# Cross-attention and a mixture of gated units on one core: first stacks by TensorE, first weights through ScalarE's queue, own slot offsets for the first half, value products by twos

## The chip, the cores and the metric

The kernel runs on one core of one Trainium2 chip. TensorE (PE) multiplies and transposes, VectorE (DVE), ScalarE (ACT) and GpSimd (POOL) do the element-wise work, and DMAs are issued here from SyncE's queue (SP), after the change from ScalarE's as well. Each engine runs its own list of instructions in order and waits on semaphores. The metric is the device time of one execution in microseconds (us), lower is better.

## The reference

One layer on x (4 batches of 512 tokens, 512 features), in float32. First attention: 16 query heads of 32 features in 4 groups, each group with one key and value head read from a 128-wide context; the queries come from the normalised x, both sides go through an RMS norm and a rotary embedding, the mask is causal, and the result is projected and added to x. Then a mixture: a router picks 4 of 128 experts per token, eight gated units are mixed with the experts' weights, two shared units are added, all goes through a down projection and is added again.

```python
q, k = _rms_norm(q, q_norm_w), _rms_norm(k, k_norm_w)      # then split into heads
q = q * cos + _rotate_half(q) * sin                        # k likewise
scores = einsum('bgnqd,bgkd->bgnqk', qg, k) * scale        # causal, then softmax
x = x + (attn @ v) @ w_out.T
gate, up = xt @ w_gate, xt @ w_up                          # 8 units of 256 columns, 2 shared
basis = silu(gate) * up                                    # mixed over the 4 chosen experts
x = x + mixed @ w_down + shared
```

## The kernel before

The program is written by hand on a grid of **slots**, from FIRST = -32 to LAST = 236. Each engine's function loops over the slots and issues, in a fixed order within a slot, the steps that tables of numbers assign to it. Nothing is scheduled at run time: the order of an engine is this list, and a late semaphore holds up all that stands behind it.

**Attention** is cut into spans `u`: a batch, a half of 256 queries (h = 0 or 1) and one of the 4 key heads, 32 spans in all. A span of half 0 takes 4 slots and has 2 steps over keys, one of half 1 takes 6 to 8 slots and has 4 steps. The constants `CORE` give each step of a span its slot, counted from the span's first.

- *Preparation.* A tile n is one 128-wide block of 256 tokens, keys first and then four query tiles for each half (n = 0 keys, n = 1 to 4 the queries of spans u = 0 to 3, n = 5 the keys of half 1, and so on). POOL (for the first two tiles partly DVE, `rope_start`) weighs it and makes the rotary parts r1_b and r2_b; POOL adds them (`rope_last`, L669); PE turns the tile by two transposes (`turn_in`, L1177); ACT rounds the turned tile to its high part (`turned_high`, L752); DVE takes the low part, the rest (`turned_low`, L933).
- *Stacking.* The scores are computed with three products in one, so each head needs its high, high and low rows (keys: high, low, high) one above the other in 96 rows of q_st or k_st. `stack_keys` (L490) and `stack_queries` (L500) do this with 12 DMAs a tile on SP's queue.
- *First pass* (`pass_a`, L1205): 8 score tiles, whose row minimum (scores are negated) DVE takes (L945) and whose exponentials ACT sums (L766). The maxima are split, turned and moved by 2 DMAs into rows 96 and 97 of q_st (`rows`, L508); rows 96 and 97 of k_st are ones (`memset`, L877).
- *Second pass* (`pass_b`, L1217 and L1220), transposed scores with the maxima subtracted, ACT's exponential (L781) into one of 3 buffers, then `value_product` (L1232): four heads at a time, 32 columns of the array each.
- `q_st` has 3 buffers, so `stack_queries(u)` waits for the second pass of u-3.

**The fillers** are the large products of projection, units and down projection (L1299, L1314, L1334), one per slot from slot 20 on. Their weights come in chunks of 1 MB into 3 buffers by DMAs on SP's queue, and are split into high and low parts by ACT (L738), DVE (L1000) and, for one block in four, POOL (L699).

**SP's queue** also carries all loads and stores. The first three chunks, the router's weights and two small tables are issued behind the query stack of u = 0; the second batch's context and x and the resident weights behind that of u = 2.

Of the kernel before, what the change touches and what calls it, by code (L numbers as in the profile page):

```python
# [13 lines left out]
CORE = dict(split=-1, inverse=2, maxima=0, spread=4, second_pass=3, inverse_turn=5,  # L14
            values=5, high=1)
# [3 lines left out]
PREP = dict(key_squares=(-31, -8), key_scale=(-24, -2), query_scale=(-24, 2), key_rope=(-21, 2),  # L19
            key_turn=(-18, 5), key_stack=(-16, 8))  # L20
SPLIT = dict(high=(3, 2), low=(2, 1))
MOMENTS = (-30, -29, -4, -4)
CONTEXT = -46
# [4 lines left out]
TILE_AT = dict(scales=(1, 3), normalize=(2, 4), turn_x=(4, 5), route=(6, 7))  # L28
PAIR_AT = dict(choose=8, keep=9, coefficients=9, turn_choice=10, mix=12)
# [20 lines left out]
def attention_and_mixture_kernel(nc, x, ctx_in, q_norm_w, k_norm_w, w_out, w_router, w_units, w_down,  # L50
# [31 lines left out]
    H = 2  # L82
# [5 lines left out]
    W8, W9 = NK, NK + 1  # L88
    POOL_LOW = (3,)
# [8 lines left out]
    with common:  # L98
# [29 lines left out]
        th, gb = sb("th", [P, 2, I]), sb("gb", [P, 2, I])  # L128
        d_h, d_l = sb("d_h", [P, 2, ND * P], F32R), sb("d_l", [P, 2, ND * P], F32R)
# [35 lines left out]
        s_tab = sem("tables_landed")  # L165
# [83 lines left out]

        def of_span(s, name):  # L250
            return spans.get(s - CORE[name])

        def second_pass_step(s):
            for u in range(NU):
                k = s - span_slot(u) - CORE["second_pass"]
                if 0 <= k < steps(u):
                    return u, k
            return None

        def value_step(s):  # L260
            for u in range(NU):
                k = s - span_slot(u) - CORE["values"]
                if 0 <= k < steps(u):
                    return u, k
            return None

        def attended_in(s):
            step = value_step(s)
            return step[0] if step and step[1] == steps(step[0]) - 1 else None
# [9 lines left out]
        def of_query(s, name):  # L279
            for u in range(NU):  # L280
                if s == span_slot(u - 2) + QUERY[name]:
                    return u
            return None
# [10 lines left out]

        spans = {span_slot(u): u for u in range(NU)}
# [49 lines left out]
        def keys_in(u):  # L345

            b, h, kv = span(u)
            c = b * KV + kv
            return [(s_k[c % KR][i], 48 * (c // KR + 1)) for i in range(h + 1)]

        def queries_in(u, j):
            return s_q[u % QR][j], 48 * (u // QR + 1)
# [7 lines left out]
        def stacked(n):  # L360

            hb, i = n // NB, n % NB
            if i == 0:
                c = hb // H * KV
                return [(s_k[(c + j) % KR][hb % H], 48 * ((c + j) // KR + 1)) for j in range(KV)]
# [48 lines left out]

        def short_products(s):

            found = []
            if (u := of_query(s, "turn")) is not None:
                found.append(("turn", query_tile(u)))
            if (hb := of_half(s, "key_turn")) is not None:  # L420
                found.append(("turn", hb * NB))
# [5 lines left out]
            if (u := of_span(s, "inverse_turn")) is not None:  # L427
                found.append(("inverse", u))
            if (g := mixture(s, "turn_x")) is not None:
                found.append(("x", g))  # L430
            if (g := turned_down(s)) is not None:
                found += [("down", 2 * g), ("down", 2 * g + 1)]
            found += [("scores", u * G * TH + m) for u, m in first_pass_tiles(s)[1:]]
            if (p := routing(s, "turn_choice")) is not None:
                found.append(("choice", p))
            if (p := routing(s, "mix")) is not None:
                found.append(("mix", p))
# [12 lines left out]
        def short_free(kind, i):  # L450
# [4 lines left out]
            return short_read[shorts[n][0]], shorts[n][1] + 1  # L455
# [3 lines left out]
        def sync_engine(e):  # L459
# [11 lines left out]

            def load_chunk(i):
                p, w = chunks[i]
                if i >= WR:
                    e.wait_ge(*chunk_read(i - WR))
                src = w_out if w == "wo" else shared_w_down if w == "ws" else w_units[w]
                for h in range(2):
                    e.dma_start(w_raw[:, i % WR, 2 * h:2 * h + 2, :], src[:, 2 * h:2 * h + 2, :]
                                ).then_inc(s_chunk[i % WR][h], 16)
# [37 lines left out]
            for t in range(TT):  # L517
                e.dma_start(x1[:, t, :], x[0, t * P:(t + 1) * P, :]).then_inc(s_x0[t], 16)
                if t == 1:
                    e.dma_start(cos_t[:], rope_cos.rearrange("(t p) d -> p t d", p=P)).then_inc(s_tab, 16)  # L520
                    e.dma_start(sin_t[:], rope_sin.rearrange("(t p) d -> p t d", p=P)).then_inc(s_tab, 16)
                    e.dma_start(wk_b[:], k_norm_w.partition_broadcast(P)).then_inc(s_tab, 16)
                    e.dma_start(wq_b[:], q_norm_w.partition_broadcast(P)).then_inc(s_tab, 16)
            for s in slots:
                if (hb := of_half(s, "key_stack")) is not None:
                    stack_keys(hb)
                for i in range(WR, len(chunks)):
                    if s == chunk_slot[i - WR] + 2:
                        load_chunk(i)
# [7 lines left out]
                for b in range(2, B):  # L537
                    if s == batch_slot(b) + CONTEXT:
                        load_ctx(b)
                if (u := of_query(s, "stack")) is not None:  # L540
                    stack_queries(u)
                    if u == 0:
                        load_chunk(0)
# [901 lines left out]
```

## Time and profile before

| | us |
|---|---|
| median of 3 runs | 898.04 (895.24 to 898.12) |
| the profiled execution | 898.34 |
| its span, first to last instruction | 896.3 |
| PE busy | 812.5 (91%) |
| DVE busy | 647.9 (72%) |
| ACT busy | 576.3 (64%) |
| POOL busy | 503.3 (56%) |

The span is what the trace covers; 2.0 us of the profiled execution lie around it. Busy is the time in which an engine has an instruction under way. Instructions on SP are issues of DMAs: the time of one is that of issuing, not of the transfer.

### The profile page before, as it was taken

To read this page: it belongs to the slowest core of one execution; us is meant where nothing else is said; L and a number is where in the kernel's file an instruction comes from. 1 tells how busy PE (TensorE), PEld (TensorE's weight loads), DVE (VectorE), ACT (ScalarE), POOL (GpSimd) and SP (SyncE) were. 2 spreads that over 40 slices of the span, in tenths; PEclk is the share of its full clock that TensorE was granted. 3 is DMA by queue.
4 is the path that set the end of the run, shared out by engine and by line. 5 is a ranking of instruction groups with operands and counts; after the bars stand their busy time and mean duration, and the time that the engine had idled before them with its cause. 6 is when DMAs were issued, how large, how long until landed. Compare 5 with 4: busy or idle time off the path is not lost. (4 is left out here: it accounts for less than half of the span.)

```text
span 896.3 us, 15336 instructions
## 1 busy us (share of the span) xinstructions
PE 812.5 (91%) x4224; PEld 602.1 (67%) x4224; DVE 647.9 (72%) x1627; ACT 576.3 (64%) x1412; POOL 503.3 (56%) x686
## 2 busy tenths in 40 slices
PE   0276978999999999999999999999999999999997
PEld 0143556767777687666777677767777777778885
DVE  3234676778887886688877786777878776678674
ACT  0265687767777676567687675667687775555452
POOL 6634551896348851797338952797345532662471
PEclk9975788999999999999999999999999999999999
DMA  3543113444453454554544453454444444454551
GB/s 95 191 128 92 58 48 112 156 140 140 153 170 123 163 159 150 174 182 136 162 145 143 163 162 128 150 171 137 160 147 144 146 141 149 158 188 141 191 192 41
DMA packets 60163, 128.37 MB, mean 143 GB/s; under 512 B 12848, under 2 KB 31152, under 8 KB 60080
## 3 DMA queue, kind: packets, MB, share of 16 engines
q1 hardware_dynamic: 60080, 127.39, 43.6%
q8 instruction: 36, 0.59, 0.3%
q14 instruction: 47, 0.39, 0.1%
HBM read 107.16 MB, written 4.19 MB: 124 GB/s over the span
## 5 line engine op out<-in xcount | busy, mean ns | idle before, releaser
L1314 PE MATMUL u<-w_h,t_h 128*128 128x512 f32 x640 | 260.7, 407 | 6.4 <-POOL w_l L699 5.6
L1314 PE MATMUL u<-w_h,t_l 128*128 128x512 f32 x640 | 251.5, 393 | 0.0
L1314 PE MATMUL u<-w_l,t_h 128*128 128x512 f32 x640 | 251.2, 393 | 0.0
L1000 DVE TENSOR_TENSOR w_l<-w_raw,w_h 128x512 fp32r<-128x512 f32 x288 | 246.0, 881 | 0.0
L738 ACT ACTIVATE w_h<-w_raw 128x512 fp32r<-128x512 f32 x384 | 219.1, 621 | 20.8 <-DMA w_raw<-in_w_units 20.2
L699 POOL TENSOR_TENSOR w_l<-w_raw,w_h 128x512 fp32r<-128x512 f32 x96 | 140.7, 1465 | 132.3 <-ACT w_h L738 131.9
L945 DVE CUSTOM_DVE_ANT_0 scores<-s,mask_qk 128x128 f32<-128x128 f32 (+3 forms) x256 | 123.5, 487 | 105.0 <-PE s L1205 102.9
L766 ACT ACTIVATE scores<-scores,mx 128x128 f32<-128x128 f32 (+3 forms) x256 | 142.4, 558 | 74.9 <-DVE mx L945 73.5
L707 POOL TENSOR_TENSOR macc<-macc,gb 128x256 f32<-128x256 f32 x112 | 103.7, 926 | 72.1 <-DVE gb L1101 71.2
L1314 PEld LDWEIGHTS u<-w_h,t_h 128*128 128x128 f32 x640 | 121.6, 190 | 32.5 <-POOL w_l L699 8.6
L1314 PEld LDWEIGHTS u<-w_h,t_l 128*128 128x128 f32 x640 | 120.7, 189 | 26.7
L1314 PEld LDWEIGHTS u<-w_l,t_h 128*128 128x128 f32 x640 | 121.3, 189 | 21.3
L1205 PE MATMUL s<-k_st,q_st 96*128 96x256 f32 (+2 forms) x256 | 102.9, 415 | 17.5 <-issue 16.6
L781 ACT ACTIVATE pr<-pair 128x1024 f32<-128x1024 f32 x96 | 84.3, 878 | 31.1 <-PE pair L1220 26.0
L828 ACT ACTIVATE th<-u 128x256 f32<-128x256 f32 x160 | 59.7, 373 | 55.0 <-PE u L1314 54.2
L1082 DVE SCALAR_TENSOR_TENSOR th<-th,u 128x256 f32<-128x256 f32 x160 | 66.7, 417 | 38.3 <-ACT th L828 37.8
L675 POOL TENSOR_TENSOR o_l<-att,o_h 128x256 fp32r<-128x256 f32 x32 | 25.8, 807 | 121.2 <-ACT o_h L786 121.2
L1205 PEld LDWEIGHTS s<-k_st,q_st 96*128 96x128 f32 x256 | 52.8, 211 | 54.8 <-issue 49.9
L1217 PE MATMUL pair<-q_st,k_st 98*128 98x512 f32 x160 | 64.3, 458 | 18.3 <-DMA q_st<-m_t 11.8
L1101 DVE SCALAR_TENSOR_TENSOR gb<-th,wt,u 128x256 f32<-128x256 f32 x112 | 53.9, 481 | 16.3 <-DVE th L1082 0.5
L1232 PE MATMUL o_bank<-pr,ct 128*32 128x256 f32 (+1 forms) x768 | 57.5, 373 | 0.0
L766 ACT ACTIVATION_READ_ACCUMULATOR scores<-scores,mx 128x1 f32 x256 | 48.7, 190 | 0.0
(139 smaller groups left out, 1148.6 us busy)
## 6 DMA issues: line engine op xcount, KB each, us to landing
w_raw<-in_w_units SPq DMA_DIRECT2D x160, 512.0 KB, 4.2
q_st<-turned_h SPq DMA_DIRECT2D x256, 32.0 KB, 1.9
w_raw<-in_w_out_t SPq DMA_DIRECT2D x16, 512.0 KB, 4.0
w_raw<-in_shared_w_down SPq DMA_DIRECT2D x16, 512.0 KB, 4.6
q_st<-turned_l SPq DMA_DIRECT2D x128, 32.0 KB, 1.9
out<-x SPq DMA_DIRECT2D x16, 256.0 KB, 2.0
x<-in_x SPq DMA_DIRECT2D x3, 1024.0 KB, 5.9
k_st<-turned_h SPq DMA_DIRECT2D x64, 32.0 KB, 1.9
```

The costliest lines, as they stand in the source:

```text
L699: e.tensor_tensor(w_l[:, i % WR, k, :], w_raw[:, i % WR, k, :], f32(w_h[:, i % WR, k, :]), ALU.subtract).then_inc(s_wlp, 1)
L707: e.tensor_tensor(total, total, gb[:, adds_before(w, g) % 2, :], ALU.add).then_inc(s_acc, 1)
L738: e.activation(w_h[:, i % WR, k, :], w_raw[:, i % WR, k, :], ACT.Copy).then_inc(s_wh, 1)
L766: e.activation(s, s, ACT.Exp, bias=mx[:, u % 2, t, j:j + 1], scale=-1.0, accum_out=sums[:, u % 2, t, j:j + 1]).then_inc(s_sum, 1)
L781: e.activation(pr[:, n % PR, 0:width], pair[:, 0:width], ACT.Exp, scale=-1.0).then_inc(s_ex, 1)
L828: e.activation(th[:, n % 2, :], u_bank[filler_no[f] % 2][:, 0:I], ACT.Tanh, scale=0.5).then_inc(s_tanh, 1)
L945: e.tensor_tensor_reduce(scores[:, i % AR, 0:width], short("scores", i)[:, 0:width], mask_qk[:, T - width:T], 1.0, 3e38, ALU.add, ALU.min, ...
L1000: e.tensor_tensor(w_l[:, i % WR, k, :], w_raw[:, i % WR, k, :], f32(w_h[:, i % WR, k, :]), ALU.subtract).then_inc(s_wl, 1)
L1082: e.scalar_tensor_tensor(th[:, n % 2, :], th[:, n % 2, :], 1.0, up, ALU.add, ALU.mult).then_inc(s_ga, 1)
L1205: e.matmul(short("scores", i)[:, 0:w], q_st[0:MAXROW, u % QR, j, t * P:(t + 1) * P], k_st[0:MAXROW, (b * KV + kv) % KR, 0:w], start=True, ...
L1217: last = e.matmul(dst, k_st[:, (b * KV + kv) % KR, k * P:(k + 1) * P], q_st[:, u % QR, i * n:(i + 1) * n, Q - w:Q], start=True, stop=True)
L1314: last = e.matmul(u_bank[n % 2][:], t[:, k, cols], ww[:, i % WR, k, :], start=(k == 0 and m == 0), stop=(k == KC - 1 and m == 2))
```

## The change

- **First stacks by TensorE.** For tiles n = 0 to 3 (`U0 = 3`: keys of half 0 and the queries of u = 0, 1, 2) POOL's last addition goes; DVE adds r1_b and r2_b and writes the sum three times side by side (`rope_stacked`, 768 elements a partition). PE makes 8 transposes of 96 columns (`turn_stacked`), which come out stacked in two banks. ACT copies each bank into q_st or k_st (`stacked_high`), DVE overwrites the low rows (`stacked_low`, two subtractions). The 12 DMAs of each of these tiles are gone, and readers wait for `s_tl` instead.
- **Queues.** The first three chunks, router, resident weights and the small tables are issued by ACT, after x's second tile has landed. SP issues k_norm_w before the tables, has own semaphores for it and q_norm_w, and issues the second batch's context and x at once, the third's x at slot 15.
- **Offsets.** Spans of the first half (u < 4) take their slots from `LEAD`, others from `CORE`, of which `inverse`, `spread` and `values` change. Some numbers of `PREP`, `MOMENTS`, `TILE_AT` and `PAIR_AT` move by a few slots. The ones of k_st are set at slot -9 and not first.
- **Value products by twos** (`value_products`): two steps over keys follow each other directly, in the slot in which the second of them stood before (in the first half of batch 0, in the slot of the first). Their semaphore rises by 2 at the end of the pair.
- Within a slot the steps stand in another order on PE, ACT, DVE and POOL, and the second of two tiles that read the same chunk no longer waits for the chunk's splitting.

```diff
-CORE = dict(split=-1, inverse=2, maxima=0, spread=4, second_pass=3, inverse_turn=5,
-            values=5, high=1)
+CORE = dict(split=-1, inverse=1, maxima=0, spread=2, second_pass=3, inverse_turn=5,
+            values=6, high=1)
+
+LEAD = dict(split=-1, inverse=0, maxima=1, spread=0, second_pass=3, inverse_turn=3, values=5, high=0, rope=-11, turn=0, stack=-3)
...
+CONTEXT, ONES = -44, -9
+ROPE3 = (-20, -11, -6, -4)
+LOADS = (-1, 15)
...
+        def queries_in(u, j):
+            if u < U0:
+                return s_tl, u + 2
+            return s_q[u % QR][j], 48 * sum(i % QR == u % QR for i in range(U0, u + 1))
...
+            def stacked_high(n):
+                e.wait_ge(s_turn, n + 1)
+                for i in range(2):
+                    last = e.activation(stack_of(n, i), short("stack", 2 * n + i)[0:MAXROW, :].rearrange(
+                        "p (j q) -> p j q", j=2), ACT.Copy)
+                last.then_inc(s_th, 1)
...
+            def rope_stacked(n):
+                e.wait_ge(*cosined(n))
+                e.wait_ge(s_rs, n + 1)
+                if n >= 2:
+                    e.wait_ge(s_turn, n - 1)
+                parts = (part.rearrange("p t (h d) -> p (t h) d", d=D).unsqueeze(2).broadcast_to([P, TH * G, 3, D])
+                         for part in (r1_b[:, n % 2], r2_b[:]))
+                e.tensor_tensor(r3[:, n % 2], *parts, ALU.add).then_inc(s_rope, 1)
...
+            def stacked_low(n):
+                rows = slice(D, 2 * D) if n == 0 else slice(2 * D, 3 * D)
+                e.wait_ge(s_th, n + 1)
+                for i in range(2):
+                    low = stack_of(n, i)[rows]
+                    last = e.tensor_tensor(low, short("stack", 2 * n + i)[rows, :].rearrange("p (j q) -> p j q", j=2),
+                                           f32(low), ALU.subtract)
+                last.then_inc(s_tl, 1)
...
+            def turn_stacked(n):
+                e.wait_ge(s_rope, n + 1)
+                e.wait_ge(s_mask, 1)
+                for i in range(2):
+                    e.wait_ge(*short_free("stack", 2 * n + i))
+                    bank = short("stack", 2 * n + i)
+                    for j in range(2):
+                        for t in range(TH):
+                            copies = r3[:, n % 2, t * G + 2 * i + j].rearrange("p c d -> p (c d)")
+                            last = e.transpose(bank[0:MAXROW, j * Q + t * P:j * Q + (t + 1) * P], copies, ident[:])
...
-            def value_product(u, k):
+            def value_products(u, first):
                 b, h, kv = span(u)
-                n, w = step_no(u, k), Q - seen(u, k)
-                e.wait_ge(s_ex, n + 1)
-                if k == 0:
+                if first == 0:
                     e.wait_ge(s_att, u)
...
+                for k in (first, first + 1):
+                    n, w = step_no(u, k), Q - seen(u, k)
+                    e.wait_ge(s_ex, n + 1)
...
+                last.then_inc(s_pv, 2)
```

On SP's queue, the stretch from the query stack of u = 2 to that of u = 3, before. `q_st<-m_t` are the rows of maxima.

```order
L500 DMA q_st<-turned_l 32x256
L508 DMA q_st<-m_t 1x4x256 [waits max_out]
L508 DMA q_st<-m_t 1x4x256
L500 DMA q_st<-turned_h 32x256 [waits turned_low]
L500 DMA q_st<-turned_h 32x256
L500 DMA q_st<-turned_l 32x256
```

The same queue after, from the last loads at the start to the first keys that still go by DMA (those of half 1).

```order
L512 DMA ct<-in_ctx 128x4x128
L518 DMA x<-in_x 128x4x512
L548 DMA q_st<-m_t 1x4x256 [waits max_out]
L548 DMA q_st<-m_t 1x4x256
L540 DMA q_st<-turned_h 32x256 [waits pass_b,turned_low]
L540 DMA q_st<-turned_h 32x256
L540 DMA q_st<-turned_l 32x256
```

The first stacks by DMA are now those of u = 3, behind the first rows of maxima and behind a wait for the second pass of u = 0; before, four tiles and all loads stood ahead of them.

On DVE, from the second tile's cosine part to the first row minimum, before (`ISA` of L888 is a sum of squares, that of L945 the row minimum).

```order
L927 TENSOR_TENSOR r_b<-rw_b,csq 128x256 [waits q_tables_dve,weighed_dve]
L933 TENSOR_TENSOR turned_l<-s,turned_h 128x256 [waits turned_high]
L888 ISA junk,ssk<-ct 128x128 [waits key_squares,ctx0_landed]
L888 ISA ssk 128x1
L888 ISA junk,ssk<-ct 128x128 [waits key_squares,ctx0_landed]
L888 ISA ssk 128x1
L933 TENSOR_TENSOR turned_l<-s,turned_h 128x256 [waits turned_high]
L945 ISA scores,mx<-s,mask_qk 128x128 [waits masks_set,pass_a]
```

The same place and what follows it, after (L987 is the cosine part, L999 the threefold addition, L1011 the low rows, L1024 the row minimum).

```order
L987 TENSOR_TENSOR r_b<-rw_b,csq 128x256 [waits q_tables_dve,weighed_dve]
L1011 TENSOR_TENSOR k_st<-s,k_st 32x2x256 [waits turned_high]
L1011 TENSOR_TENSOR k_st<-s,k_st 32x2x256
L999 TENSOR_TENSOR r<-r_b 128x768 [waits sine,cosine_dve]
L936 MEMSET k_st 2x3072
L1011 TENSOR_TENSOR q_st<-s,q_st 32x512 [waits turned_high]
L1011 TENSOR_TENSOR q_st<-s,q_st 32x512
```

```order
L1024 ISA scores,mx<-s,mask_qk 128x128 [waits masks_set,pass_a]
L1024 ISA mx 128x1
L1011 TENSOR_TENSOR q_st<-s,q_st 32x512 [waits turned_high]
L1011 TENSOR_TENSOR q_st<-s,q_st 32x512
L1024 ISA scores,mx<-s,mask_qk 128x256 [waits masks_set,pass_a]
L1024 ISA mx 128x1
L999 TENSOR_TENSOR r<-r_b 128x768 [waits turned,sine,cosine_pool]
```

The low rows and the additions of the next query tiles now stand between the row minima of u = 0, each behind a wait for PE and ACT.

On PE, in the last two slots of a span of half 1, before: two steps of value products with a score tile between them.

```order
L1232 MATMUL o_bank<-pr,ct 32x256 x4
L1205 MATMUL s<-k_st,q_st 128x384
L1232 MATMUL o_bank<-pr,ct 32x128 x4
L1205 MATMUL s<-k_st,q_st 128x512
```

After, the same two steps.

```order
L1308 MATMUL s<-k_st,q_st 128x512
L1336 MATMUL o_bank<-pr,ct 32x256 x4
L1336 MATMUL o_bank<-pr,ct 32x128 x4
L1308 MATMUL s<-k_st,q_st 128x384
```

They now stand next to each other.

## Rows read from the trace of the kernel before

**Rows 1.** The page: PE's busy share, in tenths, in 40 slices of the span.

```profile
PE   0276978999999999999999999999999999999997
```

**Rows 2.** Busy time by stretch: us, PE, PEld, DVE, ACT, POOL, PEclk, DMA, GB/s.

```profile
60.00:70.00 10.00, 8.24 (x36) 4.45 (x36) 4.45 (x23) 6.33 (x22) 1.56 (x4) 0.50 0.20 52
...
200.00:300.00 100.00, 98.18 (x532) 73.52 (x530) 81.94 (x207) 74.14 (x184) 61.16 (x84) 1.00 0.47 154
```

**Rows 3.** The timeline of SP, 42 to 91 us: start, us, line, tiles.

```profile
42.39 1.36 SPq L508 DMA_DIRECT2D q_st<-m_t  x2
...
54.49 1.20 SPq L500 DMA_DIRECT2D q_st<-turned_h  x2
...
70.18 1.29 SPq L508 DMA_DIRECT2D q_st<-m_t  x2
...
79.17 0.58 SPq L469 DMA_DIRECT2D x<-in_x  x1
79.85 1.28 SPq L508 DMA_DIRECT2D q_st<-m_t  x2
...
90.17 1.28 SPq L508 DMA_DIRECT2D q_st<-m_t  x2
```

**Rows 4.** The timeline of PE where the second passes start, 60 to 100 us.

```profile
72.65 0.79 PE L1217 MATMUL pair<-q_st,k_st 98*128 98x512 f32 x1 [3.65 <-DMA q_st<-m_t]
...
98.61 1.19 PE L1217 MATMUL pair<-q_st,k_st 98*128 98x512 f32 x2 [2.06 <-ACT pr L781]
```

**Rows 5.** The timeline of all engines, 3 to 35 us.

```profile
10.24 0.23 DVE L907 TENSOR_TENSOR csq<-cos_t,sc 128x64 f32<-128x64 f32 x1 [3.64 <-DMA wq_b<-in_q_norm_w]
...
13.05 0.69 PE L1177 MATMUL s<-ident,r_b 128*128 128x128 f32 x2 [13.05 <-POOL r_b L669]
...
25.48 0.77 PE L1205 MATMUL s<-k_st,q_st 96*128 96x256 f32 x2 [3.14 <-issue]
...
34.12 0.37 ACT L758 ACTIVATE m_t<-s 8x256 fp32r<-8x256 f32 x1 [0.62 <-PE s L1185]
```

**Rows 6.** The same view, 75 to 115 us: second pass, splitting of weights, low parts.

```profile
85.56 0.80 PE L1217 MATMUL pair<-q_st,k_st 98*128 98x512 f32 x1 [3.21 <-DMA q_st<-m_t]
...
94.23 1.14 ACT L738 ACTIVATE w_h<-w_raw 128x512 fp32r<-128x512 f32 x2
...
94.74 1.05 PE L1217 MATMUL pair<-q_st,k_st 98*128 98x512 f32 x2
...
95.72 1.66 DVE L1000 TENSOR_TENSOR w_l<-w_raw,w_h 128x512 fp32r<-128x512 f32 x2
...
114.90 0.69 DVE L1014 TENSOR_TENSOR t_l<-s,t_h 128x512 fp32r<-128x512 f32 x1 [0.54 <-ACT t_h L799]
```

**Rows 7.** The timeline of PE around value products and without them, 606 to 621 us.

```profile
606.98 0.39 PE L1299 MATMUL u<-w_h,o_l 128*128 128x512 f32 x1
607.29 0.43 PE L1232 MATMUL o_bank<-pr,ct 128*32 128x128 f32 x8
607.65 0.38 PE L1205 MATMUL s<-k_st,q_st 96*128 96x256 f32 x1
607.87 0.40 PE L1314 MATMUL u<-w_h,t_h 128*128 128x512 f32 x1
...
609.02 0.39 PE L1314 MATMUL u<-w_h,t_l 128*128 128x512 f32 x1
...
609.37 0.40 PE L1314 MATMUL u<-w_h,t_h 128*128 128x512 f32 x1
...
619.58 0.39 PE L1314 MATMUL u<-w_h,t_l 128*128 128x512 f32 x1
...
620.69 0.38 PE L1194 MATMUL s<-ident,rrep 128*128 128x128 f32 x2
```

**Rows 8.** One line's instructions over 95 to 896 us: the value products.

```profile
L1232 PE MATMUL o_bank<-pr,ct x704: 272/379/636, 103.7 to 770.8; 128*32 128x256 f32 x120, 128*32 128x128 f32 x56
```

**Rows 9.** Waits of PE over the span: us in total, times, longest.

```profile
PE u L1314 <- POOL w_l L699: 5.6, 7, 1.7
```

More of the change, by code:

```diff
@@ L258, in second_pass_step, with value_steps, attended_before @@
             return None
-        def value_step(s):
+        def value_steps(s):
             for u in range(NU):
-                k = s - span_slot(u) - CORE["values"]
-                if 0 <= k < steps(u):
-                    return u, k
+                for k in range(0, steps(u), 2):
+                    if s == span_slot(u) + core(u, "values") + k:
+                        return u, k
             return None
         def attended_in(s):
-            step = value_step(s)
-            return step[0] if step and step[1] == steps(step[0]) - 1 else None
+            found = value_steps(s)
+            return found[0] if found and found[1] == steps(found[0]) - 2 else None
+        def attended_before(s):
+            for u in range(NU):
+                if s == span_slot(u) + core(u, "values") + steps(u) - 2 + core(u, "high"):
+                    return u
+            return None
         def first_pass_tiles(s):
@@ L348, in keys_in, with keys_half_in @@
             c = b * KV + kv
-            return [(s_k[c % KR][i], 48 * (c // KR + 1)) for i in range(h + 1)]
+            return [keys_half_in(c, i) for i in range(h + 1)]
+        def keys_half_in(c, h):
+            if c < KV and h == 0:
+                return s_tl, 1
+            earlier = range(KV if h == 0 else 0, c + 1)
+            return s_k[c % KR][h], 48 * sum(i % KR == c % KR for i in earlier)
         def queries_in(u, j):
-            return s_q[u % QR][j], 48 * (u // QR + 1)
+            if u < U0:
+                return s_tl, u + 2
+            return s_q[u % QR][j], 48 * sum(i % QR == u % QR for i in range(U0, u + 1))
         def max_rows(u):
@@ L411, in evicted, with stacks @@
             return gated(w, g)
+        def stacks(n):
+            return [("stack", 2 * n), ("stack", 2 * n + 1)] if n <= U0 else [("turn", n)]
         def short_products(s):
             found = []
[L418 to L421, printed above, removed]
             if (u := of_span(s, "maxima")) is not None:
@@ L454, in short_free, with stack_of, load_chunk @@
                 return s_mask, 1
-            return short_read[shorts[n][0]], shorts[n][1] + 1
+            kind, i = shorts[n]
+            return (s_tl, i // 2 + 1) if kind == "stack" else (short_read[kind], i + 1)
+        def stack_of(n, i):
+            if n == 0:
+                return k_st[0:MAXROW, 2 * i:2 * i + 2, 0:Q]
+            return q_st[0:MAXROW, n - 1, 2 * i:2 * i + 2, :]
+        def load_chunk(e, i):
+            p, w = chunks[i]
+            if i >= WR:
+                e.wait_ge(*chunk_read(i - WR))
+            src = w_out if w == "wo" else shared_w_down if w == "ws" else w_units[w]
+            for h in range(2):
+                e.dma_start(w_raw[:, i % WR, 2 * h:2 * h + 2, :], src[:, 2 * h:2 * h + 2, :]
+                            ).then_inc(s_chunk[i % WR][h], 16)
         def sync_engine(e):
@@ L876, in vector_engine, with ones @@
         def vector_engine(e):
-            e.memset(f32(k_st[MAXROW:ROWS, :, :]), 1.0).then_inc(s_ones, 1)
+            def ones():
+                e.memset(f32(k_st[MAXROW:ROWS, :, :]), 1.0).then_inc(s_ones, 1)
             def key_squares(hb):
```

276 lines of the change are left out of this document (154 added, 122 removed).

## The prediction

> **What bounds the kernel now.** I read four views. The 40 slices of the span first: PE is nearly idle at the start, half busy in slices 3 to 5 and at 9 tenths from slice 6 on [rows 1]. Each slice is 22.4 us, so there are two regimes. Then the busy times by stretch: from 200 to 300 us PE has 98.18 of 100 us at clock 1.00, the others 61 to 82; from 60 to 70 us it has 8.24 of 10 at clock 0.50, the lower of its two levels, 1.2 GHz [rows 2]. From about 100 us on PE's own stream is the bound. Before that something else is.
>
> What, is in SP's timeline. From the first key stack to the rows of span 4 SP issues one DMA after another, about 0.6 us each (two in 1.20 to 1.36), back to back but for the last microsecond. The rows of maxima of spans 0, 2, 3 and 4 are issued at 42.39, 70.18, 79.85 and 90.17 [rows 3]. Those of span 0 had been ready in m_t since 34.12 + 0.37 = 34.5 [rows 5]: they stood 8 us behind weights and stacks. PE in turn waits for exactly these rows in its second passes, 3.65 us at 72.65 and 3.21 at 85.56 [rows 4, 6]. The head is bound by SP's issuing. How long rows take to arrive depends on what was queued: 2.5 us from 70.18 to 72.65, 5.7 us from 79.85 to 85.56 with a load of x issued just before, at 79.17 [rows 3, 4, 6].
>
> **The head.** The change takes 48 stacking DMAs (4 tiles of 12) and the first weights off SP. It doesn't follow that their 30 us go, since in their place comes a chain through four engines, and I follow it.
>
> Keys. PE began to turn them at 13.05 [rows 5]. DVE now adds 768 elements where POOL added 256. No row shows that. Two additions of 512 elements took 1.66 us [rows 6], 0.83 each; 768 cost between that and 1.5 times it, and I take 1.2. PE starts at about 13.4. Eight transposes for two: two took 0.69 [rows 5]; four times that is 2.8, but they overlap, so I take 2.0. ACT's two copies of 512 columns take 1.14 as the two of the weights [rows 6], DVE's two low parts read a bank as the row of 0.69 does [rows 6], 1.3. With gaps the keys are complete at 18.2. Before, twelve issues of 0.6 us, 7.6 us, followed the turn.
>
> Queries of span 0. Their addition stands on DVE behind the keys' low rows: 18.2 + 1.2 + 2.0 + 1.2 + 1.3 and gaps gives 24.3. The first score tile came at 25.48 [rows 5] and now comes at about 24.5. The chain thus gives back nearly all that the DMAs cost. The ones of k_st (2.6 us of DVE) are now set while PE and ACT turn this tile, so they cost nothing as long as that takes 3.2 us; uncovered they would cost 2.6. The loads that moved: x, context and weights are some 5 MB that now start in the first 12 us. In the profile DVE waited 3.64 us for q_norm_w, to 10.24 [rows 5]. It is now needed at about 13.8, so contention has 3 us to use up before it costs. ACT's ten issues, at 0.6 each and behind x's second tile, end by 13, before its first copy at 15.5.
>
> First pass of span 0. On DVE the order now puts span 1's low rows behind the first row minimum, span 2's addition behind the second and span 2's low rows into span 1's first pass. Each waits for addition, PE, ACT in turn, 4.5 us and gaps. From 24.5: sums of squares and addition to 27, low rows of span 1 done at 31.6, addition to 33, six row minima and a moment to 37, the turn of span 2 (its bank must be free) 38, low rows 40.7, and only then the maxima's transposes, which need that bank: m_t at 42. Before it was 34.5. **The rows of span 0 leave at 42.3 where they left at 42.39.** Bounds: if none of this lies between, the maxima follow the first tile by 34.5 - 25.5 = 9.0 us as before, 33.5; if nothing overlaps, 46.
>
> From there the gain begins. No load is under way, so these rows arrive in 2.5 us (bound 5.7). The second pass of span 0 takes some 4 us with one exponential in between, and releases the stacks of span 3, which wait for it: at 48.8, where they began at 54.49 [rows 3]. From here to the rows of span 4 SP has the same 36 us in both: 48 stacks at 0.635, three pairs of rows at 1.4, one load; before, 90.17 - 54.49 = 35.7. So they leave at 84.5, not 90.17. The load of x now stands right before them, so I give them the slow 5.3 to 5.7 us, and the second pass of span 4 begins at about 90, not 94.74 [rows 6]. **Term: -5 us**; from -14 (33.5 for 42.3) to 0 (46, or a slow landing).
>
> The Trainium skill, page "DMA: Bandwidth & Descriptors", section "Issuing engines are not separate DMA queues", says that issuing from another engine saves only the time to initiate a DMA, usually small against the transfer. Here rows 3 show that time, 0.6 us a piece without a gap, as the bound of the head. By the page the head would give nothing.
>
> **Value products by twos.** Between a product's last matmul at 606.98 and the next unit's at 607.87 lie 0.89 us with a value step and one score tile; with the score tile alone, 609.02 to 609.37, it is 0.35 [rows 7]. So a step of 128 columns costs 0.54. One of 256 costs 620.69 - 619.58 - 0.35 = 0.76 [rows 7]. Twice the columns cost 0.22 more, so some 0.3 us of every step are not columns: entering and leaving the narrow tiles. From 95 us on there are 704 / 8 = 88 steps [rows 8], afterwards 44 pairs, and each pair enters and leaves once: 44 x 0.3 = 13 us. The eight steps before 95 us lie beside SP and give nothing. No row shows two steps side by side, so the bounds are 0 (each step still pays) and 14.
>
> The page "TensorEngine Tiling (Array Packing)", section "Key Properties", of the Trainium skill says that changing the tiling mode, not just the tile, drains TensorE. That would make the cost one of the pair. By it the sum is the 13 us; if every new tile paid, it would be 0.
>
> Not all of it arrives. PE also waits after 100 us, mostly short and for others: 5.6 us in 7 waits for POOL's w_l in the units [rows 9]. What PE wins just ahead of such a wait, the wait takes back. **Term: -11 us.**
>
> **The rest.** The orders within a slot, the slots of choose, turn_x, inverse and spread, and the dropped waits move work on engines that are 61 to 82% busy beside PE at 98% [rows 2]. I set them at 0. The slack of a slot (3.6 us) covers each; uncovered, one such place costs what POOL's longest wait does, 1.7 us [rows 9]. PE idles 1.8 us in 100 there [rows 2], so some 14 us in 800 are to be had, or to be added to: -6 to +6.
>
> **Sum.** 898.3 of the profiled execution - 5 - 11 = 882.3; it stands 0.3 above the median, so 882.
>
> **Rivals.**
> *The chain hides* (0.20). PE may have turned to its upper clock level by the first stacks, which shortens eight transposes to about 1 us each time, and DVE may overlap more. Then the rows of span 0 leave at 33.5 to 38 and the head gives 10 to 14: 898.3 - 14 - 11 = 873. Against it: at 60 to 70 us PE, much busier, still had 0.50 [rows 2].
> *The head gives nothing* (0.15), which is what the page on DMA would say: the chain ends at 46 or the loads delay a norm weight: 887.
> *Pairs don't pay* (0.13): the drain belongs to each step, or waits take the gain: 893 with the head's 5.
> *Slower* (0.06). The exponential of a span's fourth step writes the buffer of its first, which is released only with the pair, one slot later than before; the next second pass waits for that exponential. PE lost 2.06 us in such a wait at 98.61 [rows 4]. The 16 us of gain are gone from the eighth such stall; one in each of the 16 spans of half 1 costs 33: 898.3 - 16 + 33 = 915. Against it: the pair stands early in the slot, the exponential late.
>
> **Numbers.** The forecast, 877 to 888, has 0.42. 868 to 893 leaves out the far end of the first rival (0.06) and what is above (0.12), and takes in the bounds of head and pairs one at a time. 0.3% is what a measurement can tell from no change, 2.7 us: faster by more 0.90 (the forecast and three rivals), within it 0.04 (pairs and head both without effect), slower 0.06.
>
> **What would show it.** Rows of span 0 leaving SP near 42 us, stacks of span 3 near 49, the rows of span 4 near 84 and PE dense from 95 instead of 100. In value products, sixteen matmuls together and 0.3 us less in each pair. Wrong would be: rows of span 0 before 38 (head too small), a gap between the two steps of a pair, or new PE waits for `pr` or w_l of more than 2 us that recur with the batch.

## The result and the profile after

The change makes the kernel faster: 876.39 us (median of 4 runs, 875.83 to 878.02) against 898.08 us; the ratio is 0.9768, with a 95% interval of 0.9744 to 0.9792. That is 20.8 us less by the ratio, where 16 were forecast; 876.4 lies inside the range of 868 to 893 and below the forecast's own 877. The profiled execution took 878.02 us, with a span of 876.2.

The page of the kernel after answers to [rows 1]: PE's busy share in 40 slices of 21.9 us.

```profile
span 876.2 us, 15366 instructions
...
PE   1566789989999998989999999998999999999997
```

PE now works in the first slice and is at 9 from the seventh on, with a few 8s among them, where before the steady 9 began with the eighth. The first projection (88.59, below) still comes only at the end of the fourth slice. The prediction reads slices 3 to 5 of [rows 1] as half busy and a 9 from the sixth on; they show 7, 6 and 9. No term of its sum rests on that.

SP's timeline after, 39 to 83 us, answers to [rows 3] (L548: rows of maxima, L540: query stacks, L518: load of x).

```profile
39.41 1.36 SPq L548 DMA_DIRECT2D q_st<-m_t  x2
46.17 1.22 SPq L540 DMA_DIRECT2D q_st<-turned_h  x2
...
54.64 1.28 SPq L548 DMA_DIRECT2D q_st<-m_t  x2
...
81.47 0.58 SPq L518 DMA_DIRECT2D x<-in_x  x1
82.18 1.27 SPq L548 DMA_DIRECT2D q_st<-m_t  x2
```

The rows of span 0 leave at 39.41 (before 42.39), the stacks of span 3 at 46.17 (before 54.49), the rows of span 4 at 82.18 (before 90.17). Between the last two it took 36.0 us, before 35.7, but the two are not made of the same. Before there were two pairs of rows between and SP stood idle for 1.4 us ahead of the rows of span 4, whose maxima ACT finished only at 90.15. After there are three pairs and next to no gap, and these maxima had been ready since 80.44, 1.7 us before their turn. The lines are SP's last stack and ACT's copy of the maxima before, then ACT's copy after.

```profile
88.16 0.59 SPq L500 DMA_DIRECT2D q_st<-turned_l  x1
89.79 0.36 ACT L758 ACTIVATE m_t<-s 8x256 fp32r<-8x256 f32 x1
```

```profile
80.08 0.36 ACT L801 ACTIVATE m_t<-s 8x256 fp32r<-8x256 f32 x1
```

The timeline of DVE after, 11 to 37 us, shows the chain that took the DMAs' place (L999: threefold addition, L936: the ones, L1011: low rows).

```profile
11.48 0.96 DVE L999 TENSOR_TENSOR r<-r_b 128x768 f32<-128x768 f32 x1 [1.62 <-POOL r_b L697]
...
16.86 1.28 DVE L1011 TENSOR_TENSOR k_st<-s,k_st 32x512 fp32r<-32x512 f32 x2 [3.17 <-ACT k_st L793]
18.17 0.96 DVE L999 TENSOR_TENSOR r<-r_b 128x768 f32<-128x768 f32 x1
19.83 2.62 DVE L936 MEMSET k_st<- 2x3072 f32 x1 [0.70 <-issue]
22.48 1.29 DVE L1011 TENSOR_TENSOR q_st<-s,q_st 32x512 fp32r<-32x512 f32 x2
...
28.56 1.29 DVE L1011 TENSOR_TENSOR q_st<-s,q_st 32x512 fp32r<-32x512 f32 x2 [2.00 <-ACT q_st L793]
...
36.73 1.29 DVE L1011 TENSOR_TENSOR q_st<-s,q_st 32x512 fp32r<-32x512 f32 x2 [1.84 <-ACT q_st L793]
```

And PE's timeline of the same stretch and up to the first filler, with the stack of transposes (L1280), score tiles (L1308), second passes (L1320) and the projection (L1404).

```profile
12.49 1.95 PE L1280 MATMUL s<-ident,r 128*96 128x128 f32 x8 [12.49 <-DVE r L999]
...
23.87 0.55 PE L1308 MATMUL s<-k_st,q_st 96*128 96x256 f32 x1 [2.74 <-DVE q_st L1011]
...
41.96 0.79 PE L1320 MATMUL pair<-q_st,k_st 98*128 98x512 f32 x1 [0.49 <-DMA q_st<-m_t]
...
57.09 0.80 PE L1320 MATMUL pair<-q_st,k_st 98*128 98x512 f32 x1 [5.94 <-DMA q_st<-m_t]
...
87.30 1.17 PE L1320 MATMUL pair<-q_st,k_st 98*128 98x512 f32 x2 [2.47 <-DMA q_st<-m_t]
88.27 0.52 PE L1308 MATMUL s<-k_st,q_st 96*128 96x384 f32 x1
88.59 0.63 PE L1404 MATMUL u<-w_h,o_h 128*128 128x512 f32 x1
...
91.00 0.63 PE L1320 MATMUL pair<-q_st,k_st 98*128 98x512 f32 x2
```

The first score tile comes at 23.87 (before 25.48), the second pass of span 4 at 87.30 (before 94.74).

For the kernel before, the same view shows the first projection at 99.60, behind a second pass that had waited for the exponential:

```profile
99.60 0.63 PE L1299 MATMUL u<-w_h,o_h 128*128 128x512 f32 x1
```

So of the 20.1 us between the two spans, 7.4 are won up to the second pass of span 4, 3.6 between that and the first projection (4.9 us before, 1.3 after), and 9.1 from there to the end. The 3.6 are not all gain. The wait for the exponential that is gone took 2.06 of them; the other 1.5 are work that now stands behind the first projections and no longer ahead of them, above all the two matmuls of the second step, at 98.61 before [rows 4] and at 91.00 after. So some 2 us were won there and 10.6 behind it.

A pair of value products after, between a score tile and a unit, answers to [rows 7]:

```profile
587.77 0.28 PE L1308 MATMUL s<-k_st,q_st 96*128 96x256 f32 x1
587.98 0.86 PE L1336 MATMUL o_bank<-pr,ct 128*32 128x256 f32 x16
588.77 0.50 PE L1420 MATMUL u<-w_h,t_h 128*128 128x512 f32 x1
589.11 0.39 PE L1420 MATMUL u<-w_l,t_h 128*128 128x512 f32 x1
```

Sixteen matmuls stand in one group. From 587.77 to 589.11 it is 1.34 us; a score tile and a unit's matmul alone take 0.35 ([rows 7]), so both steps cost 0.99, where a step of each size on its own cost 0.54 + 0.76 = 1.30. A pair is 0.31 us cheaper, as computed from one place of each kernel. The waits in the units, answering to [rows 9], from 100 to 870 us:

```profile
PE u L1420 <- POOL w_l L735: 7.6, 5, 2.7
PE u L1420 <- DVE gb L1180: 3.3, 1, 3.3
...
PE u L1404 <- POOL w_l L735: 2.2, 2, 1.5
```

PE waits longer for POOL than before: 7.6 for 5.6 us in the units. The longest two of these waits are

```profile
394.80 0.80 PE L1420 MATMUL u<-w_h,t_h 128*128 128x512 f32 x1 [2.67 <-POOL w_l L735]
...
593.93 0.50 PE L1420 MATMUL u<-w_h,t_h 128*128 128x512 f32 x1 [2.68 <-POOL w_l L735]
```

They stand 199 us apart, and the longest in the units before was 1.7 us [rows 9].

### The profile page after: what moved, and what is told of

Its sections match the earlier page's. It is cut to its first block, busy times and chain, and to the rows that moved or that the text cites. A ratio compares the mean times of both kernels' runs of the same rounds, so it can differ in the third digit from the quotient of the medians.

```text
span 876.2 us, 15366 instructions
## 1 busy us (share of the span) xinstructions
PE 803.1 (92%) x4248; PEld 614.5 (70%) x4248; DVE 655.1 (75%) x1635; ACT 576.3 (66%) x1416; POOL 502.6 (57%) x682
## 4 chain that ended last, share of the span: by engine, by line
PE 60%; POOL 14%; SPq 6%; issue 6%; DVE 6%; ACT 3%; DMA 3%; ACTq 1%; POOLq 0%; DVEq 0%
PE u L1420 36%; PE u L1441 7%; SPq L540 4%; PE pair L1320 3%; PE o_bank L1336 3%; PE s L1308 3%; POOL macc L743 3%; POOL w_l L735 2%; PE u L1404 2%; POOL r_b L697 2%; PE pair L1323 1%; PE s L1356 1%; PE s L1388 1%; DVE w_l L1079 1%; DMA w_raw<-in_w_units 1%
## 5 line engine op out<-in xcount | busy, mean ns | idle before, releaser
L1420 PE MATMUL u<-w_h,t_h 128*128 128x512 f32 x640 | 267.1, 417 | 11.5 <-POOL w_l L735 7.6
L1079 DVE TENSOR_TENSOR w_l<-w_raw,w_h 128x512 fp32r<-128x512 f32 x288 | 248.7, 890 | 0.9 <-ACT w_h L774 0.9
L735 POOL TENSOR_TENSOR w_l<-w_raw,w_h 128x512 fp32r<-128x512 f32 x96 | 134.8, 1404 | 130.4 <-ACT w_h L774 130.2
L1024 DVE CUSTOM_DVE_ANT_0 scores<-s,mask_qk 128x128 f32<-128x128 f32 (+3 forms) x256 | 123.4, 486 | 87.9 <-PE s L1308 85.6
L743 POOL TENSOR_TENSOR macc<-macc,gb 128x256 f32<-128x256 f32 x112 | 112.6, 1007 | 56.6 <-DVE gb L1180 55.9
L1308 PE MATMUL s<-k_st,q_st 96*128 96x256 f32 (+2 forms) x256 | 94.5, 380 | 12.3 <-DVE q_st L1011 5.1
L1320 PE MATMUL pair<-q_st,k_st 98*128 98x512 f32 x160 | 62.7, 448 | 11.0 <-DMA q_st<-m_t 9.3
L1308 PEld LDWEIGHTS s<-k_st,q_st 96*128 96x128 f32 x256 | 52.5, 209 | 28.2 <-issue 13.1
L711 POOL TENSOR_TENSOR o_l<-att,o_h 128x256 fp32r<-128x256 f32 x32 | 23.8, 743 | 83.2 <-ACT o_h L829 83.2
L809 ACT ACTIVATION_READ_ACCUMULATOR scores<-scores,mx 128x1 f32 x256 | 48.8, 190 | 0.0
L1336 PE MATMUL o_bank<-pr,ct 128*32 128x256 f32 (+1 forms) x768 | 47.2, 366 | 0.0
```

What stands on the lines that cost most here:

```text
L735: e.tensor_tensor(w_l[:, i % WR, k, :], w_raw[:, i % WR, k, :], f32(w_h[:, i % WR, k, :]), ALU.subtract).then_inc(s_wlp, 1)
L743: e.tensor_tensor(total, total, gb[:, adds_before(w, g) % 2, :], ALU.add).then_inc(s_acc, 1)
L809: e.activation(s, s, ACT.Exp, bias=mx[:, u % 2, t, j:j + 1], scale=-1.0, accum_out=sums[:, u % 2, t, j:j + 1]).then_inc(s_sum, 1)
L1024: e.tensor_tensor_reduce(scores[:, i % AR, 0:width], short("scores", i)[:, 0:width], mask_qk[:, T - width:T], 1.0, 3e38, ALU.add, ALU.min, ...
L1079: e.tensor_tensor(w_l[:, i % WR, k, :], w_raw[:, i % WR, k, :], f32(w_h[:, i % WR, k, :]), ALU.subtract).then_inc(s_wl, 1)
L1308: e.matmul(short("scores", i)[:, 0:w], q_st[0:MAXROW, u % QR, j, t * P:(t + 1) * P], k_st[0:MAXROW, (b * KV + kv) % KR, 0:w], start=True, ...
```

## The experiments

Each kernel was timed in turn with the kernel before on the same chip; ratios are to that. Repeated executions of one kernel differ by 0.2 to 1% here, so a milestone of a single profile is read beside the median, not for it. The kernels ran on more than one chip, where the kernel before took 897.9 to 899.2 us; differences of medians below can therefore be off by about 1 us, and where one matters the difference by the ratios stands beside it, with its 95% interval (an estimate from the two intervals).

**Value products: undone, alone, and with POOL out of the way.** The kernel `single` is that of after with single steps, the second in its place:

```diff
-            values=6, high=1)
+            values=5, high=1)
...
-                for k in range(0, steps(u), 2):
+                for k in range(steps(u)):
...
-                for k in (first, first + 1):
+                for k in (first,):
```

> The kernel after, with each value step on its own again (the first of a pair one slot earlier, the second where the pair stands). If entering and leaving the narrow tiles costs 0.3 us a step, 44 more of these after 88 us cost up to 13 us: 889. The kernel after spends 8.7 us less from the first projection on than before, so if waits swallow part, 885. If the pairs are worth nothing and the other order did it all: 876.

Measured: 882.86 us (ratio 0.9828, 0.9805 to 0.9852), 6.5 us more than after, or 5.4 by the ratios (2 to 8). It is nearer to the 885 of partly swallowed pairs than to 889. The expectation's 8.7 us from the first projection on should read 9.1. `before_pairs` is the kernel before with the two steps written together in `value_product`, at the second's slot:

```diff
+                if second % 2 == 0:
+                    return
...
+                for k in (second - 1, second):
+                    n, w = step_no(u, k), Q - seen(u, k)
+                    e.wait_ge(s_ex, n + 1)
...
-                last.then_inc(s_pv, 1)
+                last.then_inc(s_pv, 2)
```

> The kernel before, with pairs of value steps and nothing else. Pairs worth 11 us on their own: 887. If they need the other orders to be of use: within 2 us of 898. The start up to the second pass of span 4 stays at 94.7 us.

Measured: 893.81 us (ratio 0.9961, 0.9935 to 0.9987): 4 us less than before, and neither 887 nor nothing. The ten executions fall into seven from 891.7 to 894.8 and three from 898.2 to 900.5, and the profile is of one of the three; in it the second pass of span 4 begins at 94.53, as before. Both kernels say that half or less of the 13 us arrives. The waits of PE from 100 to 870 us in the profile of `single` say where the rest may be:

```profile
PE u L1420 <- POOL w_l L735: 4.5, 4, 1.9
PE u L1420 <- DVE gb L1180: 2.9, 1, 2.9
...
PE u L1404 <- POOL w_l L735: 1.4, 2, 0.7
```

With single steps PE waits 5.9 us for POOL's w_l, with pairs 9.8, and all its waits of this stretch together grow from some 21 to 26 us. To test that, the next two kernels leave POOL's low part of each chunk's fourth block out, and PE multiplies by the high part in its place; one has pairs, one single steps.

```diff
             if k in POOL_LOW:
-                return s_wlp, i * len(POOL_LOW) + sum(j in POOL_LOW for j in range(k + 1))
+                return s_wh, i * KC + k + 1
...
-                    for m, (t, ww) in enumerate(((t_h, w_h), (t_h, w_l), (t_l, w_h))):
+                    for m, (t, ww) in enumerate(((t_h, w_h), (t_h, w_h if k in POOL_LOW else w_l), (t_l, w_h))):
```

> Leaves work out: POOL no longer makes the low part of a chunk's fourth block, and TensorE multiplies by the high part in its place (same number of matmuls, another result). With pairs. PE's 9.8 us of waits for POOL's w_l go, and POOL is freer: 862 to 868. To be read against the next kernel.

> The same with single value steps. If the pairs' 13 us are partly swallowed by waits for POOL's w_l, the difference to the kernel with pairs, 6.5 us with POOL's work in place, grows to 10 to 13 here. If a pair itself is worth only half of what I computed, it stays at 6.5.

Measured: 857.99 us with pairs, 870.41 with single steps. The first is below the 862 to 868 expected. The difference is 12.4 us (10 to 15 by the ratios), where it was 6.5 with POOL's work in place. So pairs are worth nearly the 13 us computed, and POOL's low parts took about half of that back. The profiles agree in direction, with smaller numbers: from the first projection to the end pairs give 9.5 us without POOL's low parts (89.70 to 857.9 for 91.35 to 869.0) and 3.6 with them (88.59 to 876.2 for 89.65 to 880.9). Taking POOL's low parts away gave 18.4 with pairs and 12.4 with single steps, more than the waits for w_l, 9.8 and 5.9. POOL has some 135 us less to do, and behind a wait PE's matmuls run slower for a while (a filler's matmul every 0.42 us behind the wait at 394.80, every 0.23 ahead of 587.77); how the 18.4 divide between these was not tested.

**Stacks by TensorE, undone.**

```diff
-    U0 = 3
+    U0 = -1
...
-            if c < KV and h == 0:
-                return s_tl, 1
-            earlier = range(KV if h == 0 else 0, c + 1)
+            earlier = range(c + 1)
```

> The kernel after, but all stacks by DMA again (48 issues more on SP, no transposes of 96 columns). My theory: the chain through DVE, PE and ACT costs nearly what the DMAs did; rows of span 0 leave SP near 45 us for 39.4, stacks of span 3 near 51 for 46.2, the time rises by 5 us to 881. Rival: the 30 us of issuing were on the path, 900 or more.

Measured: 883.72 us (ratio 0.9831, 0.9796 to 0.9865), 7.3 more than after, or 5.7 by the ratios (2 to 10). SP's timeline of this kernel:

```profile
45.40 1.35 SPq L546 DMA_DIRECT2D q_st<-m_t  x2
...
62.35 1.28 SPq L546 DMA_DIRECT2D q_st<-m_t  x2
...
91.11 1.28 SPq L546 DMA_DIRECT2D q_st<-m_t  x2
```

The rows of span 0 leave at 45.4, as expected, 6 us later than after and not 30. The stacks of span 3 begin at 54.77, where 51 was expected, and the rows of span 4 leave 8.9 us later than after. The chain costs nearly what the DMAs did, and the theory of the head stands; its size in the total stays rough, since the profiled execution (879.53) is the fastest of four that reach 885.48, and made up most of the 9 us behind the first projection.

**Queues.** `loads_on_sp` issues the first weights and small tables from SP at the start:

```diff
-            e.wait_ge(s_x0[1], 16)
-            load_chunk(e, 0)
...
+            load_chunk(e, 0)
+            e.dma_start(rt_raw[:, :, NE:2 * NE], w_router).then_inc(s_rt, 16)
```

> The kernel after, but the first weights, router and small tables issued by SP at the start. SP is idle from about 7 to 39 us in the kernel after, so ten more issues cost nothing: 876 within 1.5. If issuing by ACT or its own queue is what helps, 880 or more.

Measured: 874.81 us (ratio 0.9738, 0.9711 to 0.9766): no loss, at most a small gain; the intervals of the two overlap. It is not ScalarE's queue that helps. Its profile shows what the issues on ACT cost in the kernel after. With the loads on SP, ACT loads its table at 0.72 and copies the keys as soon as PE has turned them:

```profile
0.72 1.28 ACT L800 ACT_TABLE_LOAD   x1 [0.72 <-PEq L1546]
15.31 1.08 ACT L800 ACTIVATE k_st<-s 96x512 fp32r<-96x512 f32 x2 [13.31 <-PE s L1279]
```

In the kernel after, the table load of 1.28 us stands behind the ten issues and begins at 14.45, just when the eight transposes end (12.49 + 1.95). The copy has to wait for it until 15.74:

```profile
14.45 1.28 ACT L793 ACT_TABLE_LOAD   x1 [14.45 <-issue]
15.74 1.08 ACT L793 ACTIVATE k_st<-s 96x512 fp32r<-96x512 f32 x2
```

So the issues on ACT put 1.3 us into the chain of the keys. With the loads on SP the first turn begins 0.84 us later (13.33), and still the first score tile comes 0.44 earlier (23.43). In `before_act_loads` the kernel before gets the change's move of the loads alone, ten issues from SP to ACT:

```diff
                     stack_queries(u)
-                    if u == 0:
-                        load_chunk(0)
-                        e.dma_start(rt_raw[:, :, NE:2 * NE], w_router).then_inc(s_rt, 16)
...
-                        load_chunk(1)
-                        load_chunk(2)
...
         def scalar_engine(e):
...
+            e.wait_ge(s_x0[1], 16)
+            load_chunk(0)
+            e.dma_start(rt_raw[:, :, NE:2 * NE], w_router).then_inc(s_rt, 16)
+            load_chunk(1)
+            e.dma_start(wd_raw[:], w_down).then_inc(s_wd, 16)
```

> The kernel before, with only the first weights, router and small tables issued by ACT at the start. SP loses ten issues, 6.5 us, ahead of the stacks of span 3. If SP's issuing is the bound of the head, these leave it near 48 instead of 54.5 and the time falls by 6 us, to 892. If the head is bound by something else, or these loads now slow the stacks, 898.

Measured: 893.40 us (ratio 0.9953, 0.9931 to 0.9974), 4 to 5 us less. The stacks of span 3 begin at 50.48, not 48. The first rows of maxima leave SP earlier by 3.4 and those of span 4 by 4.0 us:

```profile
38.97 1.34 SPq L508 DMA_DIRECT2D q_st<-m_t  x2
...
86.16 1.28 SPq L508 DMA_DIRECT2D q_st<-m_t  x2
```

The ten issues take 5.4 us on SP before (29.98 to 34.82, and one of 0.55 at 52.53), not 6.5. Of these, 1.4 are lost at the start, where the moved loads delay q_norm_w: DVE waits 5.14 us for it, where it waited 3.64 [rows 5], and the first turn begins at 14.44 for 13.05.

```profile
11.64 0.23 DVE L915 TENSOR_TENSOR csq<-cos_t,sc 128x64 f32<-128x64 f32 x1 [5.14 <-DMA wq_b<-in_q_norm_w]
```

5.4 - 1.4 is the 4.0 us by which the rows of span 4 leave earlier. It matters that the loads are issued where SP has nothing else to do, not by whom.

**What sets the end of the head.** In `rows_first` the 12 stacks of span 3 stand behind the rows of span 1:

```diff
-                if (u := of_query(s, "stack")) is not None and u >= U0:
+                if (u := of_query(s, "stack")) is not None and u > U0:
                     stack_queries(u)
+                if s == span_slot(1) + 1:
+                    stack_queries(U0)
```

> The kernel after, with the 12 stacks of span 3 behind the rows of span 1 on SP. PE's wait of 5.9 us at 57 us goes. By the theory that the sum of SP's issues from 46 us on sets the end of the head, nothing is won: the rows of span 4 still leave at 82 to 84 us, 876 within 1.5. If that wait was on the path, 871.

Measured: 874.19 us (ratio 0.9735, 0.9707 to 0.9763). Its profile has the second pass of span 1 at 49.3 instead of 57.1 us, and still the rows of span 4 as after:

```profile
81.70 1.28 SPq L548 DMA_DIRECT2D q_st<-m_t  x2
```

PE's longest wait of the head was worth 0.5 us at the end of it. The median is 2.2 us below after, 0.7 more than the expectation allowed, but the intervals of the two overlap. In `x_later` the third batch's x is out of the way:

```diff
-LOADS = (-1, 15)
+LOADS = (-1, 21)
```

> The kernel after, with the load of the third batch's x at slot 21 and not right ahead of the rows of span 4. Those arrive in 2.5 us instead of 5.1 and leave 0.7 us earlier: the second pass of span 4 at 84 for 87.3, 873. If the stretch after it is bound by ACT or POOL anyway, 876.

Measured: 876.78 us (ratio 0.9758, 0.9736 to 0.9779), no different from after. The second pass of span 4 begins 3.9 us after the issue of its rows (81.42) instead of 5.1, and without a wait, directly behind the score tiles, so that the rows had landed before:

```profile
85.34 1.05 PE L1320 MATMUL pair<-q_st,k_st 98*128 98x512 f32 x2
```

The first projection then begins at 87.09 for 88.59. The 2 us won at the second pass can't be seen in the total. `four_stacked` stacks the queries of span 3 by TensorE too:

```diff
-ROPE3 = (-20, -11, -6, -4)
+ROPE3 = (-20, -11, -6, -4, 0)
...
-    U0 = 3
+    U0 = 4
...
+                if n > QR:
+                    e.wait_ge(*second_pass_over(n - 1 - QR))
```

> The kernel after, with the queries of span 3 stacked by TensorE too (12 DMAs less on SP). The rows of span 1 leave SP right when ready, near 48 for 54.6, and the rows of span 4 near 75 to 78 for 82.2: 870. If by then the chain of DVE, PE and ACT sets the pace, 876.

Measured: 872.26 us (ratio 0.9708, 0.9677 to 0.9739). The rows of span 4:

```profile
78.38 1.28 SPq L548 DMA_DIRECT2D q_st<-m_t  x2
```

They leave 3.8 us earlier than after, and the time falls by 4.1, or 5.4 by the ratios (2 to 9): less than the 12 issues (7.6 us), since the rows of span 1 leave only at 50.12 and not at 48. Of the kernels that compute everything this has the lowest median. `four_x` is that kernel with the later load:

```diff
-LOADS = (-1, 15)
+LOADS = (-1, 21)
```

> The kernel with four query tiles' worth of stacks by TensorE (span 3 too) and the third x at slot 21. If the two gains at the start add up, the second pass of span 4 comes at 80 to 81 and the time is 870; if what follows is bound by the others, 872 as without the later load.

Measured: 874.00 us (ratio 0.9730, 0.9702 to 0.9758): nothing added, though the first projection begins at 83.31 for 84.77.

**The second pass's place in a slot.**

```diff
+                if (step := second_pass_step(s)) is not None:
+                    pass_b(*step)
                 if s in fillers:
                     product[fillers[s][0]](fillers[s], 0)
```

> The kernel after, with PE's second pass of a slot ahead of the filler's first half, as in the kernel before. The first projection then waits for the exponential of span 4's first step, some 2 us, and so may the later ones: 879. If the place in the slot does nothing, 876.

Measured: 879.32 us (ratio 0.9789, 0.9749 to 0.9829). The median is 3 us up as expected, but the interval overlaps that of after, and the four executions are two of 877 and two of 882, so the total doesn't decide. The profiled one took 876.88. It shows the other order: the projection stands behind both steps of the second pass again and begins 3.4 us after the first of them (86.58 to 90.00) instead of 1.3, with a wait of only 0.46 us for the exponential in between. PE's waits for the exponential from 100 us on grow from 1.0 us to 7.4:

```profile
PE pair L1320 <- ACT pr L824: 7.4, 3, 3.8
```

## Why the prediction was right, point by point

- **The bound of the head** was SP's issuing: right. From the stacks of span 3 to the rows of span 4 it took 36.0 us for the 35.7 forecast. That it is the same before and after is partly chance: before it was a pair of rows less and 1.4 us of idle SP, where the prediction counts three pairs for both. `four_stacked` takes twelve issues away and the rows leave 3.8 us earlier, `x_later` takes one away and they leave 0.8 earlier (0.3 of it from an earlier start), and `rows_first` shows that a wait of 5.9 us on PE in between changes nothing there.
- **The chain in the DMAs' place**: right in kind, 3 us too long. The threefold addition took 0.96 us for 1.2, the first turn began at 12.49 for 13.4, the keys were complete at 18.14 (18.2), and a query tile took 5.6 us from the start of its addition to the end of its low part (18.17 to 23.77) for some 6.1. The first score tile came at 23.87 (24.5 forecast). Most of the error lies behind it, in the interleaved tiles of the first pass: the low rows of span 1 ended at 29.9 for 31.6, the rows of span 0 at 39.41 (42.3), the stacks of span 3 at 46.17 (48.8), the rows of span 4 at 82.18 (84.5), the second pass of span 4 at 87.30 (90). The head gave 7.4 us for 5. The error of the chain, 2.9 us at the rows of span 0, is passed on nearly unchanged, as 2.3 to 2.7. `dma_stacks` confirms that the exchange is worth some 6 to 9 us and not the 30 of issuing. The rival *the chain hides* did not come: the eight transposes took 1.95 us, not 1.
- **Arrival of the rows**: right. 2.5 us from 39.41 to 41.96 with nothing else under way, 5.1 from 82.18 to 87.30 behind the load of x.
- **The loads on ACT** were to end before ACT's first copy and cost nothing: wrong, by 1.3 us of the keys' chain. Their ten issues took 8.9 us, not 6, and ended at 14.42, and the table load behind them, which the prediction doesn't have, held the copy back from 14.44 to 15.74. There was no margin left.
- **Value products by twos**: the mechanism right, the term mis-sized. 12.4 of the 13 us are there when POOL's low parts are out of the way, and I let 2 of them be lost; some 6.5 were. The step that was mis-sized is the sentence on what a wait takes back: the 5.6 us of waits in 7 places [rows 9] were taken as they stood, but they grow when PE gets faster. Waits for w_l are 3.9 us longer with pairs than without, all waits together some 5.6. One of the prediction's own signs of being wrong came true here: waits for w_l of more than 2 us that recur with the batch, at 394.80 and 593.93.
- **The rest at 0**: too low. Between the second pass of span 4 and the first projection a wait of 2.06 us went that no term had. The filler's first half now stands ahead of the second pass that waits for an exponential, the very wait that I had in [rows 4] and used only for the rival. `second_pass_first` shows longer waits for exponentials, 7.4 us from 100 us on, though not their worth in the total. Behind the first projection some 4 us more were won than the pairs explain (10.6 for 6.5). Waits for the exponential that fell from 4.4 us to 1.0 there would fit most of that, but no run tests the other orders and offsets by themselves, so the cause of this part stays open.
- **The rival of slower**, exponentials that wait for the pair: nothing of it. PE waits for `pr` only 1.0 us from 100 us on, before 4.4.
- **The two rules.** Moving the loads from ACT to SP's idle start lost nothing (`loads_on_sp`), and taking ten issues out of SP's busy stretch gave 4 to 5 us (`before_act_loads`). The Trainium skill, page "DMA: Bandwidth & Descriptors", section "Issuing engines are not separate DMA queues", says that another engine saves only the time to initiate, usually small; the first half agrees, the size doesn't where a queue of issues is the bound. For the narrow tiles, sixteen matmuls in one group saved one entry and exit, 0.31 us. The Trainium skill, page "TensorEngine Tiling (Array Packing)", section "Key Properties", has the drain at a change of the tiling mode; the pairs agree with that.

The sum, 16 for 21 us, thus came about as 5 + 11 + 0 where the runs show 7.4, about 6.5, and some 6 for orders and waits, for which there was no term. The mechanisms of head and pairs hold; that the total is as near as 5 us is in part luck, since the pairs were over-sized by 4.5 us while head and rest were under-sized by 2.4 and 6.

## What to carry to other kernels

Where a queue of issues is the bound, take the work off it by following what replaces it, engine by engine: 48 issues of 0.6 us were worth some 7 us here, since their replacement ran through three engines in turn, and a load moved to idle time of the same queue was worth as much as one moved to another engine. Look at what stands behind moved issues on the new engine too: here a table load did. Small matmuls with another tile width cost 0.3 us here at entry and exit, read from the starts of their neighbours; put them side by side. Expect a gain on the busiest engine to be shared with the engine close behind it, and test that by taking away the latter's work, not by counting its waits.

## What the runs showed of the hardware

- DVE's additions in float32 lie on one line here: 256 elements a partition took 0.42 us (L987), 512 took 0.69 (L1014 of the kernel before, one input in PSUM), 768 took 0.96 (L999), each 256 more 0.27. The 0.83 for 512 from which the prediction took its 1.2 [rows 6] is half of the one pair at 95.72; the median of all 288 instructions of that line, L1000, is 0.69 too. From it the same bounds would have been 0.69 to 1.04.
- The time of a DMA issue is not a property of the engine. The loads at the start took 0.45 to 1.33 us each on ACT, and in `loads_on_sp` SP took 2.10 us for two and 2.91 for one, where it takes 0.6 for each small stack later on:

```profile
5.51 1.08 ACTq L503 DMA_DIRECT2D w_raw<-in_w_out_t  x2
...
11.77 2.65 ACTq L503 DMA_DIRECT2D w_raw<-in_w_units  x2
```

```profile
5.25 2.10 SPq L503 DMA_DIRECT2D w_raw<-in_w_out_t  x2
...
13.37 2.91 SPq L518 DMA_DIRECT2D x<-in_x  x1
```

- The column PEclk reads 1.00 in the stretch from 20 to 30 us, in which eight transposes took 1.94 us and a score tile of 256 columns 0.55 (at 23.87) against 0.28 (at 587.77):

```profile
20.00:30.00 10.00, 3.84 (x17) 2.79 (x15) 7.70 (x15) 2.53 (x6) 5.13 (x9) 1.00 0.32 121
```

In the first 60 us of this trace the durations tell TensorE's speed, and that column doesn't.
